# Cross- and self-attention scores: from three bf16 parts on 64-row tiles to two float32r parts on 32-row tiles

## What is computed

```python
D, H = 128, 16
HD = D // H
SCALE = HD ** (-0.5)

def _attend(q, k, v):
    attn = jnp.einsum('bhnd,bhsd->bhns', q, k) * SCALE
    attn = jax.nn.softmax(attn, axis=-1)
    o = jnp.einsum('bhns,bhsd->bhnd', attn, v)
    B, _, N, _ = q.shape
    return o.transpose(0, 2, 1, 3).reshape(B, N, D)
```

## Time and profile before

| what | value |
|---|---|
| median of 3 runs | 5283.68 us |
| span of the profiled execution | 5282.2 us |
| TensorE busy | 4674.1 us, 88% |
| VectorE busy | 4160.5 us, 79% |
| ScalarE busy | 3597.9 us, 68% |
| POOL busy | 1667.0 us, 32% |
| share of the 16 DMA engines | 17.3% (main queue) |

### The profile page before, as it was taken

One profiled execution on the slowest core, in us unless ns is written; L12 is line 12 of the kernel. 1 busy time (PEld: TensorE's weight loads), 2 busy tenths in 40 slices (PEclk: granted clock), 3 DMA queues, 4 the chain that ended last, 5 costly groups with the idle time before them and its releaser, 6 DMA issues.

```text
span 5282.2 us, 123295 instructions
## 1 busy us (share of the span) xinstructions
PE 4674.1 (88%) x47956; PEld 2177.8 (41%) x47956; DVE 4160.5 (79%) x8997; ACT 3597.9 (68%) x4899; POOL 1667.0 (32%) x2339
## 2 busy tenths in 40 slices
...
GB/s 51 61 65 49 67 54 49 68 52 50 65 38 29 46 34 34 29 30 58 45 61 53 69 52 69 54 63 55 55 70 52 64 44 58 50 54 57 43 48 8
DMA packets 362976, 271.12 MB, mean 51 GB/s; under 512 B 47911, under 2 KB 325002, under 8 KB 362396
## 3 DMA queue, kind: packets, MB, share of 16 engines
q1 hardware_dynamic: 362396, 263.23, 17.3%
...
## 4 chain that ended last, share of the span: by engine, by line
PE 38%; DVE 7%; ACT 5%; issue 4%; POOL 0%; SPq 0%; DMA 0%; ACTq 0%; POOLq 0%; DVEq 0%
PE pb_obank L1027 14%; PE pb_dbank L1040 9%; PE pb_aunit L1003 6%; DVE pb_c_maxs L699 5%; ACT pb_probs L778 4%; PE pb_aunit L1081 2%; PE pb_aunit L1074 1%; PE pb_aunit L1066 1%; PE pb_dbank L1088 1%; PE pb_aunit L1114 1%; PE pb_aunit L1108 1%; PE pb_aunit L1011 1%; PE pb_aunit L1098 1%; DVE pb_c_mbf L709 1%; PE pb_aunit L1048 0%
## 5 line engine op out<-in xcount | busy, mean ns | idle before, releaser
L699 DVE TENSOR_REDUCE pb_c_maxs<-pb_dbank 128x1 f32<-128x512 f32 (+1 forms) x3584 | 2045.5, 627 | 312.2 <-PE pb_dbank L1040 293.4
L778 ACT ACTIVATE pb_probs<-pb_aunit 128x1024 f32<-128x1024 f32 (+1 forms) x1792 | 1761.6, 1024 | 276.2 <-PE pb_aunit L1003 223.8
L699 DVE TENSOR_REDUCE pa_c_maxs<-pa_dbank 128x1 f32<-128x512 f32 (+1 forms) x1792 | 1028.3, 627 | 181.5 <-PE pa_dbank L1040 167.6
L778 ACT ACTIVATE pa_probs<-pa_aunit 128x1024 f32<-128x1024 f32 (+1 forms) x960 | 937.4, 1024 | 194.9 <-PE pa_aunit L1003 160.6
L1027 PE MATMUL pb_obank<-pb_probs,pb_c_vaug 128*9 128x256 f32 x13312 | 945.6, 381 | 2.8 <-ACT pb_probs L778 0.2
L1040 PE MATMUL pb_dbank<-pb_c_kst,pb_c_qst 62*128 62x512 bf16 (+1 forms) x4096 | 760.6, 341 | 104.6 <-DVE pb_c_maxs L699 87.5
L1003 PE MATMUL pb_aunit<-pb_c_qst,pb_c_kst 64*128 64x256 bf16 x6144 | 581.2, 272 | 64.2 <-ACT pb_probs L778 40.6
L1040 PEld LDWEIGHTS pb_dbank<-pb_c_kst,pb_c_qst 62*128 62x128 bf16 x4096 | 227.7, 93 | 649.0 <-DVE pb_c_maxs L699 466.3
L1027 PE MATMUL pa_obank<-pa_probs,pa_c_vaug 128*9 128x256 f32 x6656 | 467.0, 381 | 1.3 <-ACT pa_probs L778 0.8
L1040 PE MATMUL pa_dbank<-pa_c_kst,pa_c_qst 62*128 62x512 bf16 (+1 forms) x2048 | 405.1, 348 | 44.9 <-DVE pa_c_maxs L699 21.1
L1027 PEld LDWEIGHTS pb_obank<-pb_probs,pb_c_vaug 128*9 128x9 f32 x13312 | 243.1, 89 | 372.3 <-issue 207.0
...
## 6 DMA issues: line engine op xcount, KB each, us to landing
pb_c_kst<-pb_c_ksp SPq DMA_DIRECT2D x384, 200.1 KB
pa_c_kst<-pa_c_ksp SPq DMA_DIRECT2D x192, 200.1 KB
...
pb_c_qst<-pb_c_qsp SPq DMA_DIRECT2D x384, 32.0 KB
pa_z_qst<-pa_z_qsp SPq DMA_DIRECT2D x192, 32.0 KB
pa_z_kst<-pa_z_ksp SPq DMA_DIRECT2D x192, 32.0 KB
```

What stands on the lines that cost most here:

```text
L699: dve.tensor_reduce(dst, dbank[N % RING_D][:, 0:cnt * width].rearrange("p (s c) -> p s c", s=cnt), AX.X, ALU.max).then_inc(d_free, 1)
L778: act.activation(probs[u % RING_P][0:rows].rearrange("p a i q -> p (a i q)"), src[0:rows, :], ACT.Exp, scale=HD ** -0.5).then_inc(a_free, 1)
```

## The change

Queries and keys are split into two parts instead of three: a high part, rounded to float32r when it is written, and the rest. Three products (high by high, low key by high query, high key by low query) make 24 rows; with the rows of the maxima a head takes a tile of 32 rows, and four heads lie side by side on the four tiles. A unit `S` of the first pair uses tiles 0 and 1, that of the second pair tiles 2 and 3; `M` of an even pair uses tiles 0 and 1, of an odd one tiles 2 and 3. The last block of keys takes 66 columns instead of 65 (one key twice). `T` is cut into two halves, `T` and `U`, since both halves write the same two banks: `U` waits for the first half to land and follows one `V` or `M` later where one comes next. The maxima's two parts are made by POOL, from VectorE's reduction. The table and the merging rule of phase pb have other values; those of phase pa stay.

```diff
-ROWS = 64
-MAX_ROW = 62
-K_PART = (0, 0, 0, 1, 1, 2)
-Q_PART = (0, 1, 2, 0, 1, 0)
+TILES = 4
+ROWS = P // TILES
+MAX_ROW = 30
+PARTS = 3
+K_LOW = (False, True, False)
+Q_LOW = (False, False, True)
-    tail = keys % 512
+    tail = keys % 512 + keys % 2
...
 PLACES_LAYERS23 = {
-    "lead": 0.6052,
+    "lead": 0.6078,
+    "rule": (0.222, 0.25, 0, 4),
...
-    return out
+    return second_halves(out)
+
+
+def second_halves(prog):
+
+    out, owed = [], None
+    for item in prog:
+        if owed is not None and item[0][0] not in ("V", "M"):
+            out.append(owed)
+            owed = None
+        out.append(item)
+        if owed is not None:
+            out.append(owed)
+            owed = None
+        if item[0][0] == "T":
+            owed = (("U", item[0][1]), item[1], item[2])
+    return out + ([owed] if owed is not None else [])
...
-            s.qst = [sb(f"{m}_qst{i}", [P, PAIRS, NQ], BF16) for i in range(2)]
-            s.kst = [sb(f"{m}_kst{i}", [P, PAIRS, s.keys], BF16) for i in range(2)]
+            s.qst = [sb(f"{m}_qst{i}", [P, QUADS, NQ]) for i in range(2)]
+            s.kst = [sb(f"{m}_kst{i}", [P, QUADS, s.keys]) for i in range(2)]
...
@@ block.sync
-                    for t in range(6):
-                        for par in range(2):
-                            lo = par * ROWS
-                            sp.dma_start(s.kst[w][lo + t:lo + K_ROWS:6, :, :], s.ksp[lo:lo + ROWS, K_PART[t], :]).then_inc(s.k_st, 16)
+                    for t in range(PARTS):
+                        src = s.klo if K_LOW[t] else s.khi
+                        for lo in range(0, P, ROWS):
+                            sp.dma_start(s.kst[w][lo + t:lo + K_ROWS:PARTS, :, :], src[lo:lo + ROWS, :].unsqueeze(1)).then_inc(s.k_st, 16)
...
-                    for par in range(2):
-                        at = par * ROWS + MAX_ROW
-                        sp.dma_start(s.qst[w][at:at + 2, 4 * half:4 * half + 4, :], s.mrow[half][par * 8:par * 8 + 8, :]).then_inc(s.m_st[half], 16)
+                    for tile in range(TILES):
+                        at = tile * ROWS + MAX_ROW
+                        sp.dma_start(s.qst[w][at:at + 2, 2 * half:2 * half + 2, :], s.mrow[tile * 4:tile * 4 + 4, :]).then_inc(s.m_st[half], 16)
...
@@ block.vector
-                    dve.wait_ge(s.m_neg, 2 * i + half + 1)
-                    if i:
-                        dve.wait_ge(a_full, a_done(("Rt", half), s, i - 1))
-                    dve.tensor_copy(s.mbf[half][:], s.negm[half][:]).then_inc(s.m_bf, 1)
-                    dve.wait_ge(s.m_bf, 2 * i + half + 1)
-                    dve.tensor_copy(s.mhl[half][:, :, :, 0, :], s.mbf[half][:]).then_inc(s.m_hl, 1)
-                    dve.tensor_tensor(s.mhl[half][:, :, :, 1, :], s.negm[half][:], s.mbf[half][:], ALU.subtract).then_inc(s.m_hl, 1)
...
@@ block.gpsimd
-                    pool.tensor_copy(s.ksp[:, 0, part], s.kf[:, part]).then_inc(s.k_hi, 1)
-                    pool.wait_ge(s.k_hi, done)
-                    pool.tensor_tensor(s.kf[:, part], s.kf[:, part], s.ksp[:, 0, part], ALU.subtract).then_inc(s.k_r, 1)
-                    pool.wait_ge(s.k_r, done)
-                    pool.tensor_copy(s.ksp[:, 1, part], s.kf[:, part]).then_inc(s.k_mid, 1)
-                    pool.wait_ge(s.k_mid, done)
-                    ins = pool.tensor_tensor(s.ksp[:, 2, part], s.kf[:, part], s.ksp[:, 1, part], ALU.subtract)
+                    pool.tensor_copy(s.khi[:, part].bitcast(F32R), s.klo[:, part]).then_inc(s.k_hi, 1)
+                    pool.wait_ge(s.k_hi, len(s.groups) * i + tok[1] + 1)
+                    ins = pool.tensor_tensor(s.klo[:, part], s.klo[:, part], s.khi[:, part], ALU.subtract)
...
+                elif k == "Rn":
+                    half = tok[1]
+                    pool.wait_ge(s.m_neg, 2 * i + half + 1)
+                    if i:
+                        pool.wait_ge(a_full, a_done(("Rt", half), s, i - 1))
+                    pool.tensor_copy(s.mhl[half][:, :, :, 0, :].bitcast(F32R), s.negm[half][:]).then_inc(s.m_hl, 1)
+                    pool.wait_ge(s.m_hl, 2 * (2 * i + half) + 1)
+                    pool.tensor_tensor(s.mhl[half][:, :, :, 1, :], s.negm[half][:], s.mhl[half][:, :, :, 0, :], ALU.subtract).then_inc(s.m_hl, 1)
...
@@ block.tensor
-                            lo = par * ROWS
-                            ins = pe.matmul(dst[:, par * 512 + h * NQ:par * 512 + (h + 1) * NQ], s.kst[b2][lo:lo + ROWS, pair, t * P:(t + 1) * P],
-                                            s.qst[b2][lo:lo + ROWS, pair, :], start=True, stop=True)
+                            lo = (2 * pp + par) * ROWS
+                            ins = pe.matmul(dst[:, par * 512 + h * NQ:par * 512 + (h + 1) * NQ], s.kst[b2][lo:lo + ROWS, q, t * P:(t + 1) * P].bitcast(F32R),
+                                            s.qst[b2][lo:lo + ROWS, q, :].bitcast(F32R), start=True, stop=True)
...
+                    if k == "U":
+                        pe.wait_ge(tail_half, 2 * (QUADS * i + q + 1))
...
-                            lo = par * ROWS
+                            lo = (2 * (p % 2) + par) * ROWS
...
-                            ins = pe.matmul(dbank[nd[tok, s.key, i, par] % RING_D][:, col:col + width], s.qst[b2][lo:lo + MAX_ROW, p, qt * P:(qt + 1) * P],
-                                            s.kst[b2][lo:lo + MAX_ROW, p, at:at + width], start=True, stop=True)
+                            ins = pe.matmul(dbank[nd[tok, s.key, i, par] % RING_D][:, col:col + width],
+                                            s.qst[b2][lo:lo + MAX_ROW, p // 2, qt * P:(qt + 1) * P].bitcast(F32R),
+                                            s.kst[b2][lo:lo + MAX_ROW, p // 2, at:at + width].bitcast(F32R), start=True, stop=True)
```

More of the change, by code:

```diff
@@ L16 @@
 BF16 = mybir.dt.bfloat16
+F32R = mybir.dt.float32r
 I32 = mybir.dt.int32
@@ L174 @@
 RING_P = 6
-K_ROWS = 48
+K_ROWS = PARTS * HD
 SET_ROWS = 64
@@ L394, in take @@
         if dve:
-            start = max(self.dve, self.pe + LATENCY) if k in ("M", "o") else self.dve
+            start = max(self.dve, self.pe + self.latency) if k in ("M", "o") else self.dve
             self.dve = start + dve
@@ L400, in take, with merge_maxima @@
                 self.d_free.append(self.dve)
-def merge_maxima(prog):
-    clocks, out, late, used = Clocks(), [], [], set()
+def merge_maxima(prog, rule):
+    latency, slack, most_late, most_early = rule
+    clocks, out, late, used = Clocks(latency), [], [], set()
     def put(item):
@@ L416, in merge_maxima @@
             late.append(item)
-        while late and (clocks.banks_free() <= clocks.pe + SLACK or len(late) > MAX_LATE or (tok[0] == "Rn" and any(m[1] is s for m in late))):
+        while late and (clocks.banks_free() <= clocks.pe + slack or len(late) > most_late or (tok[0] == "Rn" and any(m[1] is s for m in late))):
             put(late.pop(0))
@@ L420, in merge_maxima @@
             continue
-        if tok[0] in ("S", "T", "V", "k", "v", "h", "fc2", "ctx", "q") and not late and clocks.banks_free() <= clocks.pe + SLACK:
-            for m in range(n + 1, min(len(prog), n + 1 + MAX_EARLY)):
+        if tok[0] in ("S", "T", "V", "k", "v", "h", "fc2", "ctx", "q") and not late and clocks.banks_free() <= clocks.pe + slack:
+            for m in range(n + 1, min(len(prog), n + 1 + most_early)):
                 if m not in used and prog[m][0][0] in ("M", "kq", "Rn"):
@@ L428, in merge_maxima @@
         put(item)
-    return out
+    return second_halves(out)
[12 more added lines that the diff above has]
+    return out + ([owed] if owed is not None else [])
 def attention_phase(nc, nm, streams, cols_d, rows_d, ident_d, late_x, fill_late, places):
-    PROG = merge_maxima(stage_list(streams, late_x, places))
+    PROG = merge_maxima(stage_list(streams, late_x, places), places["rule"])
     na, nd, ns, nv, no, out_before, values_before = {}, {}, {}, {}, {}, {}, {}
```

102 lines of the change are left out of this document (50 added, 52 removed), and 9 rows, old and new, of the table PLACES_LAYERS23.

## The result

The changed kernel takes 5829.15 us, the median of 4 runs (5822.99 to 5850.75), against 5284.76 for the kernel before in the same comparison: a ratio of 1.1037, with a 95% interval of 1.1024 to 1.105. The prediction was 5161 us and a gain. It is 10% slower, outside the range and on the other side. The profiled execution has a span of 5821.1 us.

A forecast was written before the change was run, and what follows sets the result against it. TensorE, busy 91% and 93% in the two attention phases, was taken to set the pace, VectorE close behind. Terms -185 + 126 - 11 + 11 - 74 + 10 = -123 us gave 5161 us, range 5020 to 5330.

The forecast's parts named there:

- Part 1, Four tiles: TensorE matmuls: float32r streams at the bf16 price and units on different tiles run side by side, 185 us less.
- half speed: Rival, TensorE: float32r streams at half speed, as the float32 transposes do; 5971 us, chance 0.09.
- no side by side: Rival, TensorE: in-order starts or ScalarE's units keep the tiles from running side by side; 5346 us, chance 0.09.
- Part 2, Weight loads: TensorE: float32r loads cost as a transpose's, 49 ns more at 2,569 stretch starts, 126 us more; ends 0 and 259.
- The rival with float32's price: TensorE: a float32r weight load shows like a float32 product's, 259 instead of 126 us; 5294 us, chance 0.14.
- Part 3, Steps between modes: TensorE: fewer steps between row tiles and column strips, 11 us less; `U` waiting directly behind `T`, 11 us more.
- Part 4, Maxima: VectorE loses 188 us of work to POOL; half of TensorE's waits for VectorE go, 74 us less.
- The term of 10 us for POOL's lateness in pa: In pa POOL makes the maxima's parts behind the MLP's product, delaying `Rt` 0.7 us at 15 items: 10 us more.
- Part 5, Splitting: POOL drops splitting steps for keys and queries, but nothing but the copies waits for it: no change in time.
- Part 6, Table of pb: The new table of pb changes what stands where; for waits nothing, between 40 us less and 40 more.
- the mean load: Sign for part 2: TensorE's mean weight load would be about 145 ns.
- the one that was to prove the forecast wrong: Sign against the forecast: TensorE's busy time per phase no smaller than before.

## Why the prediction was wrong

The spans of the profiled executions lead from one kernel to the other: 5282 (before), 5272 (bf16, 64 rows: POOL's maxima, two parts and the table together, -10), 5588 (float32r loads, +316), 6153 (32 rows on two tiles, +565, all of it clock), 5821 (four tiles, -332). Of the last step, 0.39 x (1833 - 1246) = 230 is clock regained, so 102 is left for work side by side. In terms of the forecast: -10 + 316 - 102, and 0.39 x (1246 - 391) = 334 for the clock: 538 of the 539 us. The sum closes by its making; what was measured apart are the four steps.

**The missing term: the granted clock.** No term and no rival of the prediction names it. The kernel before showed 0.96 and 0.99 in both windows, and the sum took every duration at that clock. Cutting a matmul from 64 rows to 32 was costed at nothing ("rows do not cost"); by the price of 0.39 it cost 334 us. The Trainium skill (TensorE: Matmul & The Clock Gate, Part 1: The HAM clock gate) ties the clock to how busy the engine has been and tells of throttling after idle time. The kernel before agrees: behind the wait of 2.17 us in pa, which ends at 1072.56, the clock is at half.

```profile
1066.00:1072.50 6.50, 3.65 (x50) 1.44 (x42) 6.16 (x11) 4.16 (x7) 5.46 (x4) 1.00 0.11 28
1072.90:1076.20 3.30, 3.30 (x17) 2.02 (x16) 1.96 (x5) 0.96 (x2) 0.00 (x0) 0.50 0.05 13
```

After the change idle time does not tell where it falls: in 8 bodies of pa it fell ahead of the wait, in pb with the engine busy 19.04 of 20 us, and how many rows a matmul read decided how long it stayed low, 391 us of the span on 64 rows and 1833 on 32, with float32r on two tiles.

**Part 1, Four tiles** (-185): the bf16 price was right, the pairs keep their 0.11 us, and both rivals against it (half speed, no side by side) fall: `M` and `S` start together at 4003.30. The size was too large: about -102 with float32r. With bf16 the same working gives about -60: the profiled execution on four tiles is 100 us longer than on two of 64 rows (5372.7 - 5272.2), of which 0.39 x (763 - 348) = 162 is clock, at a mean clock of 0.967 there. A body of pb at full clock is 2 us shorter on four tiles than on two (89 against 91 us, from the windows above and the 64-row run's).

```profile
3216.00:3307.00 91.00, 86.88 (x983) 36.60 (x982) 81.26 (x177) 72.40 (x92) 26.01 (x51) 1.00 0.14 41
```

**Part 2, Weight loads** (+126): the step that failed is "I take the transpose", 144 ns. The load takes 197 to 201 ns, as the float32 product's 196, and the term was 317 us, above even the upper end of 259. What shows at the head of a stretch is 0.11 us instead of 0.05, which at the 2,569 places is 283 us; the rest was not taken apart. The rule of the Trainium skill that was weighed there (TensorE: Matmul & The Clock Gate, Weight-path perf modes, no fast load for FP32) holds for float32r, by this trace's 197 against 95 ns; the 139 us estimated from it were less than half of the 317. The rival with float32's price had this mechanism, and the time of 5294 only without the clock.

**Part 3, Steps between modes** (0 in all): not taken apart.

**Part 4, Maxima** (-74 + 10): wrong in sign, alone and in the whole. TensorE's waits for VectorE did fall to half (57.6 + 16.5 = 74 of 148), and VectorE's busy time to 4019 us, but the waits did not fall by the exchange: with VectorE's parts back in the changed kernel they are 48.7 + 18.0 + 2.5 = 69 us. And POOL is later than VectorE: in the kernel before the exchange costs 106 us, with a wait of 86.5 us for POOL in pb; in the changed kernel undoing it gains 45. The term of 10 us for POOL's lateness in pa was right by itself: 30.9 us in place of 20.3.

**Part 5, Splitting** (0): wrong, a gain of 78 us by itself. "Nothing but the copies waits for it" missed VectorE, which is slowed by POOL's steps beside it, the thing that part 4 had read from the trace itself, and the start of the first phase.

**Part 6, Table of pb** (0 +- 40): alone +9; under POOL's maxima and on 32 rows it is worth 211 us, the wait of `Rt` (53.6 us) and, for the larger part, clock.

Of the signs listed, the side-by-side start, the price of a pair, the halved waits for maxima and the lines gone from VectorE came as written; `Rt`'s wait behind the MLP came at 2.1 us on average (30.9 at 15 places) instead of some 3; the mean load did not come; and the one that was to prove the forecast wrong did: TensorE is busy 1524 of 1600 us in pa instead of 1460.
